# Field-pair products and a small MLP on one core: new plans for all engines, first layer in two parts, the gather's wait behind its first DMA

## The reference

```python
e = stack([tbl_f[ids[:, f]] for f in range(40)], axis=1)      # 2048 x 40 x 64
p, q = e[:, rowidx], e[:, colidx]                             # 780 pairs
z = einsum('bie,fie,bif->bi', p, param, q)                    # 2048 x 780
h = concatenate([z, dense_ctx], axis=1)                       # 2048 x 796
h = maximum(h @ W_top1 + b_top1, 0.0)                         # 512
h = maximum(h @ W_top2 + b_top2, 0.0)                         # 256
y = h @ W_top3                                                # 2048 x 1
```

## Time and profile before

| | |
|---|---|
| median of 3 runs | 1176.03 us (1175.66 to 1178.72) |
| the profiled execution | 1177.51 us |
| its span, first to last instruction | 1175.7 us |
| PE, DVE, ACT, POOL busy | 98%, 91%, 89%, 63% |
| granted TensorE clock, mean | 0.999 |
| DMA | 80.32 MB, 68 GB/s |

### The profile page before, as it was taken

The page is one execution under the profiler, slowest core; times in us unless marked ns, Lnnn a source line. Parts: engine busy times, 40 slices in busy tenths (PEclk is TensorE's granted clock), DMA queues, the critical chain, the costliest instruction groups (busy, mean ns, idle before and its releaser), DMA issues. The chain is left out here.

```text
span 1175.7 us, 22395 instructions
## 1 busy us (share of the span) xinstructions
PE 1158.0 (98%) x5490; PEld 419.5 (36%) x5490; DVE 1073.3 (91%) x964; ACT 1042.8 (89%) x8077; POOL 745.2 (63%) x803
## 2 busy tenths in 40 slices
PE   8999999999999999999999999999998999999999
PEld 3333333333334333333333333333333333333333
DVE  8599999999999999999999998999998988989970
ACT  7399989999599999999789999999988989999651
POOL 6766776567767567657767867686677576626410
PEclk9999999999999999999999999999999999999999
DMA  4243323223222222224222222222222222211200
GB/s 120 54 126 100 79 74 79 66 77 73 65 77 53 57 69 73 63 76 136 64 78 65 52 69 64 73 73 66 76 65 65 57 64 58 57 49 54 56 10 1
DMA packets 50868, 80.32 MB, mean 68 GB/s; under 512 B 13817, under 2 KB 14073, under 8 KB 50481
## 3 DMA queue, kind: packets, MB, share of 16 engines
q1 hardware_dynamic: 31016, 58.65, 16.3%
q0 software_dynamic: 19712, 20.22, 9.3%
q10 hardware_dynamic: 8, 0.01, 0.0%
HBM read 78.82 MB, written 0.01 MB: 67 GB/s over the span
## 5 line engine op out<-in xcount | busy, mean ns | idle before, releaser
L543 ACT ACTIVATE prods<-prods 128x64 f32<-128x64 f32 x3952 | 953.8, 301 | 43.9 <-DVE prods L675 42.5
L543 ACT ACTIVATION_READ_ACCUMULATOR prods<-prods 128x1 f32 x3952 | 882.2, 248 | 0.0
L675 DVE TENSOR_TENSOR prods<-ring,kept 128x1024 f32<-128x1024 f32 x428 | 495.9, 1226 | 31.8 <-PE ring L787 31.7
L452 POOL DMA_INDIRECT stage<-tbl,idx x384 | 363.5, 947 | 193.7 <-issue 159.5
L675 DVE TENSOR_TENSOR prods<-ring,emb 128x1024 f32<-128x1024 f32 x372 | 431.0, 1230 | 31.6 <-PE ring L781 30.9
L786 PE MATMUL ring<-raw,emb 64*128 64x512 f32 x856 | 420.7, 614 | 0.8
L787 PE MATMUL ring<-raw,emb 64*128 64x512 f32 x856 | 421.3, 615 | 0.0
L780 PE MATMUL ring<-emb,raw 64*128 64x512 f32 x744 | 366.8, 614 | 3.2 <-ACT emb L505 1.5
L781 PE MATMUL ring<-emb,raw 64*128 64x512 f32 x744 | 367.3, 616 | 0.0
L452 POOL DMA_INDIRECT kept<-tbl,idx x232 | 219.7, 947 | 120.6 <-issue 92.7
L786 PEld LDWEIGHTS ring<-raw,emb 64*128 64x128 f32 x856 | 142.3, 186 | 240.3 <-issue 122.9
(11 more groups left out here) (55 smaller groups left out, 318.8 us busy)
## 6 DMA issues: line engine op xcount, KB each, us to landing
raw<-param_b SPq DMA_DIRECT2D x200, 256.0 KB
stage<-tbl,idx POOLq DMA_INDIRECT x384
kept<-tbl,idx POOLq DMA_INDIRECT x232, 2.5
W<-W1g SPq DMA_DIRECT2D x2, 1792.0 KB
prods<-tbl SPq DMA_DIRECT2D x6, 224.0 KB
W<-W2t SPq DMA_DIRECT2D x1, 512.0 KB
idx<-ids_t SPq DMA_DIRECT2D x1, 240.0 KB, 5.9
prods<-tbl SPq DMA_DIRECT2D x6, 26.0 KB
```

The lines of the kernel that those rows point to most:

```text
L452: pool.indirect_dma_start(to[:, t, E * (f % 2) : E * (f % 2) + E], None, tables[f], bass.IndirectOffsetOnAxis(ap=idx[:, c, f, t : t + 1], ...
L543: op = act.activation(part, part, ACT.Copy, accum_out=sums[:, t, at : at + 1])
L675: dve.tensor_tensor(prods[:, PROD_AT[n], :, :], ring[:, n % RING, :, :], by, ALU.mult).then_inc(prod_done, 1)
```

## The change

All five plans are written anew. Three constants change, the groups of the first layer are cut in a part of four matmuls and one of three (with other work between them, `aux` kept), and the wait between gathers stands before the second DMA in every chunk. The matmuls, multiplies and gathers are the same in number.

| | before | after |
|---|---|---|
| units by DVE (d), ACT (a), POOL (p) | 121, 247, 60 | 108, 248, 72 |
| h1 parts in PE_PLAN | 12 of 7 matmuls | 12 of 4 and 12 of 3 |
| reduces that DVE_PLAN puts beside an h1 part | 4 (ten), 2 (two) | 2 at the four, 1 at the three |
| reduces beside an h2 group | 2 (five), 0 | 2 (three), 1 (two), 0 |
| bare batch sums after unit 40: without, with a reduce | 23, 47 | 21, 36 |
| sums with a duo's transposes: without, with a reduce | 2, 12 | 6, 20 |
| unit before which duos (1,9), (1,13), (3,8), (3,11), (3,12) are transposed | 224, 267, 618, 630, 642 | 228, 273, 620, 653, 669 |

```diff
 PE_PLAN = (
-    "dd..d.d...ds..dbsbb.....d......d........s...d...s....d...s.....d...s.....d...s...s....d....s...d...."
+    "dd..d.d...ds..dbsbb.....d..........d....s....sd........sd........s.d.......s...d...s......sd........"
...
 DVE_PLAN = (
-    "...........................r......r.......r........r........r...r........r........r........r........"
+    "........................r...r....r........r.r.......r........r......r......r........r..........r...."
...
 ACT_PLAN = (
-    "xxxxxxxrxrrxrrrxrrrxrrxrrrxrrzrxrrxrrrxrrrrxrrrxrrrxrrrzrxrrrrrrrxrrrxrrrrrrrxrxrxrzrxrxxzxrxrrxrxrx"
+    "xxxxxxxrxrrrxrrrxrrrxrrrxrrxrrzrrxrrrxrrxrrrxrrxrrrxrrrrrxzrrrrrrrxrxrrrrxrrrrrrzxrxrxrrxrxrrrxzrxrr"
...
 POOL_PLAN = (
-    "gggggggggggggggfggggggggfggfggggfgfgggggggfggfgggggfggfgggfggfgfggggfgfgggfgfgggggfgggfggggfgggfgfff"
-    "fffffff"
+    "gggggggggggggfgggggggggfggggggfgfgfgfgfgffgggggggfgggggggfgfgfgfgfgfggfgggggfgfgggfgfggggfgfgfgggffg"
+    "fgffgfgffffff"
 )
...
 RING = 3
-PRODS = 17
+PRODS = 19
...
-PLACES = 18
+PLACES = 14
...
-LAYERS = [("h1", n, groups) for n in range(H1 // P) for groups in (range(NG),)]
+LAYERS = [("h1", n, groups) for n in range(H1 // P) for groups in (range(4), range(4, NG),)]
...
                 for i, (f, t) in enumerate(product((2 * d, 2 * d + 1), range(BT))):
-                    if n and i == (0 if c else 1):
+                    if n and i == 1:
                         _, landed_last, times_last = staged(*GATHERS[n - 1])
                         pool.wait_ge(landed_last, 16 * 2 * BT * (times_last + 1))
```

More of the change, by code:

```diff
@@ L54 @@
 ORDER = (
[L55 to L59, removed]
@@ L60 @@
-    "aaaa aaad f f aaad f appa f aapp f aaaa ddaa f f f f f ddaa aadd f adad f aapp f f",
-    "aaad f aaad adda aapp f f f aada f adad adad f aapp adad f ddad aaaa adda adda f aapp aadd aadd f "
-    "adpp aapp f aaaa f aaaa f appa f ppaa f pppp f aapp ppaa f f aapp f f f f adpp adaa f",
+    "f f aaaa adad aada f f ddad f adda f adaa f f aada f adda f adaa f aaad adpp adaa f f "
+    "f aaad f aada f aaaa aaaa f f f aaad aada f ddaa f f aapp f f adaa f adaa aaaa f f",
+    "f f adaa daad f aaaa f appa dada ddaa ppaa ddda ppda dppa dapp f ddda adaa f ddaa ppaa f appa f aaaa "
@@ L63 @@
+    "adad daad f f f adaa f f aaad f f aaad dapp f f ddaa aaad f f aaad dada f aada f f",
+    "f f aadd dppa aaaa f ppda f dppa daaa ppaa dppd f ppaa ddad aadd addd f adaa f aada adda ddaa appa f "
+    "aaaa aaad f aaaa aaad f f f aapp f aaaa ppaa f f f adad f f f ppaa aadd f aapp f f",
+    "aaad f aaaa adda f aapp f f aada adad appd aapp f adad ddad f aaaa adda appa aapp f aadd adpp aadd f "
+    "aapp aapp f aaaa f appa daaa f pppp f f f aapp dppa dapp f f f f f f f aaaa ppaa f",
 )
 PE_PLAN = (
-    "dd..d.d...ds..dbsbb.....d......d........s...d...s....d...s.....d...s.....d...s...s....d....s...d...."
@@ new lines @@
+    "s...d.......sd.........d.....s...t...s....sd......s........s...d.........s....s....s.....d...t....s."
+    "......d...s...s.......s....s...d...d...sd.....d....d...s.....sd.....sd.....sd.....d...st.....d...s.."
+    "...l.....l.....d......d....l.....l.....d..s.....d....t..s....l.....l.....sd.....d...s...l.....l....."
+    "d...st.....sd.....l.....s...s.....sd.....s.....s...l.....l.....sd.....s...t....s....s.....d...d....s"
+    "d.....d...s...d...s....sd...s..d.....d...d....d...s...t...s....d...l.....l.....d...s...l.....l.....d"
@@ L77 @@
+    "...d....st.....l.....l.....ds.....d....l.....l.....sd.....l.....l.....sd.....st.....s.....l.....sd.."
+    "...s......s.....s.....sd......s...t...s.....sd.....d....sd.....d...sd.....sd.....d...s.....d...d...s"
+    "...t....d...s...s....d...l.....l.....d...s...l.....l.....sd.....d...t...d...l.....s...l.....d....l.."
+    "...l.....sd.....sd.....t...l.....l.....s.....sd.....l.....s.....s...s.....t....d...s...s.....s.....s"
+    ".....s.....s.....s...."
 )
 DVE_PLAN = (
-    "...........................r......r.......r........r........r...r........r........r........r........"
@@ L81 @@
[L81 to L89, removed]
+    "........................r...r....r........r.r.......r........r......r......r........r..........r...."
+    "..........r......r....r......r........r............r....r................r..........r...r.......r..."
@@ new lines @@
+    ".r.........r......................r.....r........r.............rr.....r...............rr.....r......"
+    ".r...........r....rr.....r.....r........r...rr.....r........r.....r.....rr.....r........r..........r"
+    "...r..........r.....r.......r................r........r......r....r...r.................r......r...."
+    "...rr.....r........r...rr.....r............r.....rr.....r.....r.........rr.....r.....r.....rr.....rr"
+    ".....r.........................................r......r....................r........r.....r........."
@@ L90 @@
+    "..........r..........r...r.......rr.....r........r...rr.....r.....r..............rr.....r...r......."
+    "..rr.....r.......................r.........................r...............r........................"
+    "........"
 )
 ACT_PLAN = (
-    "xxxxxxxrxrrxrrrxrrrxrrxrrrxrrzrxrrxrrrxrrrrxrrrxrrrxrrrzrxrrrrrrrxrrrxrrrrrrrxrxrxrzrxrxxzxrxrrxrxrx"
-    "rrxrrxrrxrxrrrxrxrrxrrxrxrrrxrrxrrxrrrzrxrrxrrxrxrxrrrrxrrrrrrrxrrrrxrzrrrrxrxrrxrxrrxrzxxrxrrxrxrrx"
-    "rxrrxrxrrxrxrrrxrrxrrxrxrrrxrrrxrxrrxrrxrrzrxrxrrxrrxrrrrrrrxrrrrrxrzrrrrxrxrrxrxrrxxrxzrrxrxrxrxrxr"
@@ L96 @@
-    "rxrrxrrxrrrxrrrrrxxrxrrrxrxrrrxrzrrxrxrrxrrxrxrxrrrrrxrrxrrrrrrrrxrxzrrrrrr"
+    "xxxxxxxrxrrrxrrrxrrrxrrrxrrxrrzrrxrrrxrrxrrrxrrxrrrxrrrrrxzrrrrrrrxrxrrrrxrrrrrrzxrxrxrrxrxrrrxzrxrr"
+    "xrxrxrrxrrrrrxrxrrxrrrxrrxrrxrxrrrrrxrxrrxrzrrrxrxrrxrxrrxrrrrrxrrrrxxzrxrrxrrrrxrxrxrrxrrxzrxrxrxrx"
+    "rxrrxrrxrrrxrrxrrrrxrxrxrxrrrrxrxrrxrrrrxrxzrrxrrxrrxrxrrrrxrxrrrrrrrzxrrrxrrxrrxrxrxrxrxzrrxrrxrxrr"
+    "xrxrrrxrrrrxrxrrrrrxrxrxrxrxrrrrrxrxrrrrxrxzrrxrxrrxrrxrrrxrrxrrrrrxxzrrrrrr"
 )
 POOL_PLAN = (
-    "gggggggggggggggfggggggggfggfggggfgfgggggggfggfgggggfggfgggfggfgfggggfgfgggfgfgggggfgggfggggfgggfgfff"
@@ L101 @@
-    "fffffff"
+    "gggggggggggggfgggggggggfggggggfgfgfgfgfgffgggggggfgggggggfgfgfgfgfgfggfgggggfgfgggfgfggggfgfgfgggffg"
+    "fgffgfgffffff"
 )
 SLOT_PLAN = (
[L105 to L112, removed]
+    "ghijklmnopqrsabcdefghijklmnopqrahijkscblmnodfehijkgprqsdmnolafhgjkpicdqrsmbnafghlejicdqrosbnafghlkej"
@@ new lines @@
+    "qrcafghopbejklnmacqrfigbejphdklacqrmsfigadklobcmqrenjfgisphaenqrdlkoahpsbcenqrmjgiahpsdfbcenlkorqmag"
+    "hijspdklorfbagmqcehijsrndklpoafbcehigqmdklpjsrcafhnogbeklimqdspfhjradfpsockbeiabckondpmqglsahbdmpqck"
+    "ojnlsbdhmgrafepqickagmrojnefpqlbdsghacikrmefjnodblpqshgacikjefmrdnoblpqaghsemcijkfrdalpqnbeghsomcial"
+    "pqfjdhmosnkbacilgrfjpqedhmosknlgcdiepqrbfgklnajhmseocqrdibpkemoslnrhfgidpbemajldfgikpeocqsmfnagdjlkr"
+    "pchmbagfnidjklrepcoqhmsfbdijnaqgfhmskbdijlreapgnqmscbdikofcmqshapjbdiklrcfmoesgbdjpnaqiklrchfmogesbd"
@@ L113 @@
+    "aikqpjlfgmochrnbdesaqifjlpkgmadesorchgklpbnademqrifjsoglchbnakpfijrodmqlecsghbafkpnijromdqilknpcseog"
+    "afhmbjpqilrdckegosndilrhmafpqbjclrkmednosgbcjqilrhakmdfenobpcgsrmijlqhakedfobpcgrsnijlmahkqdefobcgpi"
 )
```

## The result

| | before | after | ratio (95% interval) |
|---|---|---|---|
| median, first comparison (4 runs each) | 1176.53 us | 1168.36 us (1167.68 to 1168.83) | 0.9926 (0.9911 to 0.9942) |
| profiled execution, its span | 1177.51, 1175.7 us | 1167.94, 1165.8 us | |
| medians later, on another chip (17 and 6 runs) | 1510.74 us | 1703.05 us | 1.1259 (1.1217 to 1.13) |
| and on one more (11 and 6 runs) | 1517.04 us | 1702.68 us | 1.1246 (1.1196 to 1.1295) |

The comparison that the prediction was made for says 8.2 us faster, against 9.0 forecast (1176.03 to 1167.0). The two last lines came at the end of the study, and they are the larger news: there is a condition in which both kernels are far slower, seen on two chips, and in it the change loses 12.5%. First the normal condition.

A forecast was written before the change was run, and what follows sets the result against it. DVE's work plus its waits for PE was taken as the bound; -13.6 + 7.1 - 5.8 + 3 = -9.3 us gave 1168.2 for the profiled execution, 1166.7 for the median, likeliest 1167, range 1158 to 1177.

The forecast's parts named there:

- Reduces, -13.6: On DVE: 12 reduces fewer on the path at 1.13 us each, moved to POOL and ACT, -13.6 us.
- Ring waits, +7.1: DVE waiting for PE's products: with fewer reduces as cover, idle time rises to 50.2 us, +7.1; bounds +1 to +11.
- The rule: DVE's idle time at a block of PE work equals PE's length - 1.13 x reduces - 1.12 us.
- Gathers, -5.8: POOL's gathers: later use and the wait behind the first DMA end late landings, -5.8 us; bound -5.8 to +2.
- Places, 0: 19 places for products and 14 for embeddings add no instructions; embedding places are freed early enough: no cost.
- ACT, +3: ACT falls some 20 us behind from unit 80 to 200, late for DVE and PE: +3 us, bounds 0 and +8.
- The walk: Going through ACT's order: the product of unit 267, needed gone before multiply 278, is 2 to 3 us late.
- The tail, 0: PE alone behind the last multiply: ACT's last reduce still ends in time, 3 us of cover, 0 us.
- A: Rival: the split of h1 frees more DVE time than the rule says, 1157.7 us; chance 0.15.
- B: Rival: ACT stalls of +7 to +10 us or a late landing eat the gain, 1173 to 1178; chance 0.13.
- C: Rival: ACT's late aux saves stop PE and its clock falls, 4.8 us per place, 1183 us; chance 0.09.
- D: Rival: the DMA ahead of the wait lengthens its predecessor's landing, so the change moves nothing; counted within B.

The follow-up runs named there:

- the experiments on h1 and on covered reduces: Changed kernel with h1 in one part again: 1193.41 us, ratio 1.0133; with ten more DVE reduces where PE does sums: 1169.42 us, ratio 0.9945.
- the split alone: Kernel before with the first layer in parts of four and three matmuls, reduces shared two and two: 1183.04 us, ratio 1.0053.
- the halves: Changed kernel with 34 of the 92 batch sums done in two halves of eight matmuls, some units apart: 1174.42 us, ratio 0.9982.
- 17 places: Changed kernel with 17 places for products instead of 19, places given out anew: 1182.43 us, ratio 1.0057.

## Why the prediction was right or wrong

The total was right in the condition it was made for, 1168.4 in a range of 1158 to 1177, and so was the bound: DVE's work and its waits for PE.

1. *Reduces, -13.6.* 108 on DVE, of 1.13 us each from start to start. As counted.
2. *Ring waits, +7.1.* The rule gave 50.2 for the new plans, the profile shows 52.3; 43.1 and 43.0 for the old ones. It held part by part: the 21 bare sums leave 16.7 us, for 16.8. The 2.1 us that are missing lie in the layers, whose h1 parts I took at 3.6 and 2.7 us where they last 3.70 and 2.84. The rule held also in the experiments on h1 and on covered reduces. It fails where blocks stand directly beside each other and share the bank (the split alone), and in chains where PE is the bound (the halves).
3. *Gathers, -5.8.* No late landing is left, and the moved wait alone took 6.9 us of DVE's waits away (49.9 to 43.0) and 7.7 of the time. A little low. A landing of 6.9 us occurred (median 2.5), outside my bound of 4.1, and PE waited for none. The bound was read from landings of 72 of the 616 DMAs, none of them issued in the 10 us behind the load of `W` at 529 us; the last section has more on this. The later use of the gathers, the other half of this term, did not do it: with the old wait the same plans wait 8.2 us.
4. *Places, 0.* Shown for `emb`. For `prods` shown from the other side, by 17.
5. *ACT, +3.* This is the step that failed: DVE waited for ACT nowhere, and 0 was measured. The walk had the reduce of unit 267 end 2 to 3 us too late for multiply 278; it ended at 404.6 us and the multiply started at 405.4, so there were 0.8 us to spare. I counted a save of `aux` at its duration of 0.63 us. Between two reduces it takes less, as ACT's timeline shows (the two rows below this list): 0.48 us from start to start. From unit 80 to unit 267 ACT does 25 such saves, which makes some 3.6 us, about what the walk was off by. That this is the reason is argued and not shown: the 165 us of the sum for units 80 to 200 were met (148.5 to 314.1 us), because three saves of `z_ps`, which the sum leaves out, took what the saves of `aux` took less. With 17 places there was nothing to spare. PE's new waits for ACT's saves lie in chunk 0 and not where I had them; DVE's idle time behind them is at most 0.8 us, part of the 52.3.
6. *The tail, 0.* 36.7 us in both.

ACT's timeline in the changed kernel, a save between two reduces:

```profile
371.40 0.59 ACT L505 ACTIVATE emb<-aux 128x512 f32<-128x512 f32 x1
371.88 0.26 ACT L543 ACTIVATE prods<-prods 128x64 f32<-128x64 f32 x1
```

What the sum left out goes the other way. A wait costs more than the profile lists. Above, reduces start at 933.80, two of them should take 2.26, and the next multiply starts at 936.59: 0.53 us late with 0.46 listed. At 21 more waits than before that is 1.5 us. So from the third multiply on the stretch should be 13.6 - 2.4 - 1.5 = 9.7 us shorter, and it is 8.4. Counting every start on DVE closes most of the 1.3 us: waits shorter than those listed, and starts that come late by less than 0.1 us, are 1.2 us more in sum than before.

That the total came out within 1.4 us of the measured one is luck in good part. Without the ACT term the sum is -12.3. The waits were 1.1 us more than forecast, the restarts cost 1.5 and these small delays with what is still open 1.3, which makes -8.4. The 1.5 us at the start, of which the change has no share, bring the spans to 9.9 us apart.

Of the rivals, A and B did not come. C named a loss of the kind met later, engines that stop and a granted clock that falls (a mean of 0.86 there), but sought it in ACT's order and priced it at 16 us; there it is 192 (1703.05 - 1510.74). That the price of the new order could depend on where or when it runs was in no case of mine. In D I took it as settled by chunk 0 that a DMA ahead of the wait disturbs nothing, and in the normal condition that was true.

The attribution was also missed in one respect. By my terms the plans (parts 1, 2 and 5) bring -3.5 us and the wait -5.8. The runs say 0.4 to 2 and 7 to 8: one moved line was the change, and the five new plans are worth little more than the error of measurement.

## What to carry to other kernels

An instruction taken off the bounding engine is worth its time only if nothing that it sits beside would have made that engine wait anyway: here the same reduce was worth 1.0 us or 0.2, so count moved work by what it covers, block by block. When a change is one line and a thousand characters of plan, run the line alone. And time a change in the order of gathers on several chips and at several times before it is kept: this one gained 0.7% in one condition and lost 12.5% in another.

## What the runs showed of the hardware that I had not expected

- On two chips the kernel before took 1511 and 1517 us instead of 1176, in all of its runs there, with DMAs issued by POOL at their usual 0.945 us each and multiplies on DVE at their usual 1.22 us. What was added is idle time, most of it beside gathers.
- There, one indirect DMA issued ahead of the landing of the gather before took DVE's busy share beside gathers from some 70% down to 28% in the stretches shown, and from 64% to 43% over the whole run.
- A landing can take 6.9 us where the median is 2.5, and it is the load beside it that marks it. The gather's DMA was issued at 531.40 us, the load of `W` (1.8 MB, the first row) at 531.49, and from 530 to 540 us the DMA engines moved 255 GB/s, for 74 in the 10 us before. The runs with the moved wait alone, with the wait moved back and with sums in halves have landings of 6.6, 7.1 and 7.3 us within 2 us of the same load, so the place of the wait is not the cause.

```profile
531.49 0.42 SPq L432 DMA_DIRECT2D W<-W1g  x1
...
531.40 0.94 POOL L452 DMA_INDIRECT kept<-tbl,idx  x1 [1.07 <-DMA kept<-tbl,idx]
```

- Eight matmuls of a sum take 0.99 us from their start to the next product (1102.80 to 1103.79), where sixteen take 1.86: half the work takes more than half the time.
